# Score products of the first attention as 64-row tiles, three products for each head

## The reference

```python
lat = layer_norm(latents, ln_lat_g, ln_lat_b)
ctx = layer_norm(context, ln_ctx_g, ln_ctx_b)
q = (lat @ Wq)                       # 16 heads of 64
k, v = jnp.split(ctx @ Wkv, 2, axis=-1)
k = apply_rope(k, cos[None, None], sin[None, None])
attn = jnp.einsum('bhnd,bhsd->bhns', q, k) * DHEAD ** (-0.5)
attn = jax.nn.softmax(jnp.clip(attn, -11.0, 11.0), axis=-1)
out = jnp.einsum('bhns,bhsd->bhnd', attn, v)
return out @ Wo + bo
```

## Time and profile before

| | |
|---|---|
| time, median of 3 runs | 3606.59 us (3606.55 to 3608.03) |
| span of the profiled execution, first to last instruction | 3601.8 us |
| instructions | 38810 |
| TensorE, products | 2645.3 us busy (73%) |
| VectorE | 2401.7 us (67%) |
| ScalarE | 1384.5 us (38%) |
| GpSimd | 1429.5 us (40%) |
| mean granted TensorE clock | 0.882 of full |
| first attention's scores | 1024 products, 295.1 us busy |

### The profile page before, as it was taken

The page is one execution under the profiler, slowest core; times in us unless marked ns, Lnnn a source line. Parts: engine busy times, 40 slices in busy tenths (PEclk is TensorE's granted clock), DMA queues, the critical chain, the costliest instruction groups (busy, mean ns, idle before and its releaser), DMA issues. The chain is left out here.

```text
span 3601.8 us, 38810 instructions
## 1 busy us (share of the span) xinstructions
PE 2645.3 (73%) x11472; PEld 1632.8 (45%) x11472; DVE 2401.7 (67%) x3617; ACT 1384.5 (38%) x1913; POOL 1429.5 (40%) x1019
## 2 busy tenths in 40 slices
PE   3987987997996867887788778777877354646465
PEld 3555554554553754544454445444544222323232
DVE  4886786787785764666466646664665586877775
ACT  2553552552552004544354425543553231313121
POOL 3663662563562012343334324432443253443434
PEclk9998998998998877999999889998999676767676
DMA  2010010010101120000000000000000100000000
GB/s 57 14 31 22 14 31 17 15 35 1 30 9 36 47 59 14 13 5 27 22 14 5 27 21 14 5 27 21 14 5 0 38 12 5 25 0 29 0 18 6
DMA packets 109968, 70.48 MB, mean 20 GB/s; under 512 B 15011, under 2 KB 109795, under 8 KB 109795
## 3 DMA queue, kind: packets, MB, share of 16 engines
q1 hardware_dynamic: 109796, 68.44, 6.4%
HBM read 60.03 MB, written 8.39 MB: 19 GB/s over the span
## 5 line engine op out<-in xcount | busy, mean ns | idle before, releaser
L726 ACT ACTIVATE cross_probs<-cross_scores 128x1024 f32<-128x1024 f32 x256 | 259.3, 1024 | 379.8 <-PE cross_scores L938 376.8
L852 DVE TENSOR_REDUCE cross_part<-cross_ring 128x1 f32<-128x512 f32 x512 | 333.0, 686 | 78.4 <-PE cross_ring L1013 75.2
L726 ACT ACTIVATE latent_probs<-latent_scores 128x1024 f32<-128x1024 f32 x256 | 259.1, 1025 | 226.1 <-PE latent_scores L938 202.9
L1013 PE MATMUL cross_ring<-cross_S,cross_Q 128*128 128x512 f32 x512 | 219.3, 475 | 152.9 <-DVE cross_part L852 77.5
L938 PE MATMUL latent_scores<-latent_Q,latent_S 128*128 128x512 f32 x1024 | 295.1, 422 | 28.2 <-issue 17.8
L938 PE MATMUL cross_scores<-cross_Q,cross_S 128*128 128x512 f32 x1024 | 297.7, 420 | 6.0 <-ACT cross_probs L726 2.6
L1046 PE MATMUL latent_outT<-latent_probs,latent_VN 128*64 128x512 f32 x1024 | 264.6, 625 | 15.5 <-DVE latent_probs L873 15.3
L1046 PE MATMUL cross_outT<-cross_probs,cross_VN 128*64 128x512 f32 x1024 | 270.4, 629 | 0.0
L482 POOL TENSOR_TENSOR cross_acc<-cross_probs 128x1024 f32<-128x1024 f32 x32 | 79.8, 2493 | 437.7 <-ACT cross_probs L726 437.7
L482 POOL TENSOR_TENSOR latent_acc<-latent_acc,latent_probs 128x1024 f32<-128x1024 f32 x64 | 153.7, 2402 | 229.0 <-DVE latent_probs L873 229.0
L938 PEld LDWEIGHTS latent_scores<-latent_Q,latent_S 128*128 128x128 f32 x1024 | 191.3, 199 | 111.9 <-issue 53.4
(11 more groups left out here) (300 smaller groups left out, 6531.7 us busy)
## 6 DMA issues: line engine op xcount, KB each, us to landing
latent_WRAW<-in_L_xattn_Wkv_dram SPq DMA_DIRECT2D x64, 128.0 KB, 2.3
latent_C<-in_ctx_dram SPq DMA_DIRECT2D x4, 1024.0 KB, 6.4
latent_WRAW<-in_L_xattn_Wq_dram SPq DMA_DIRECT2D x32, 128.0 KB, 2.3
cross_C<-in_ctx_dram SPq DMA_DIRECT2D x4, 1024.0 KB, 8.6
cross_WRAW<-in_L_xattn_Wq_dram SPq DMA_DIRECT2D x32, 128.0 KB, 2.3
cross_WRAW<-in_L_xattn_Wk_dram SPq DMA_DIRECT2D x32, 128.0 KB, 2.4
cross_WRAW<-in_L_xattn_Wv_dram SPq DMA_DIRECT2D x32, 128.0 KB, 2.3
latent_XN<-in_x_dram SPq DMA_DIRECT2D x4, 512.0 KB, 3.9
```

The lines of the kernel that those rows point to most:

```text
L726: nc.scalar.activation(probs[h][c % 2][:, :, :], scores[h][:, :, :], ACT.Exp).then_inc(exp_done, 1)
L852: nc.vector.reduce_max(part[:, h, qt, i:i + 1], bank[:, :], AX.X).then_inc(taken, 1)
L1013: nc.tensor.matmul(bank[:, :], Q1[nxt][:, h, qt * P:(qt + 1) * P], S1[nxt][:, h, i * 512:(i + 1) * 512], start=True, stop=True).then_inc(f ...
```

## The change

For the latent layer alone, S1, S2, Q1 and Q2 become tiles of 128 partitions for both heads together: high parts in S1 and Q1, low parts in S2 and Q2, head 0 on partitions 0 to 63 and head 1 on 64 to 127. One ScalarE operation copies the whole bank and one VectorE operation subtracts, for kT and for q; the second copy of the queries and the four memsets of zeros are gone. The score products of both heads are issued together at head 1's place: for each key tile three products for each head, 64 rows deep, the two heads in turn, 12 in a chunk. They wait for both exps of the chunk before. At head 0's place the latent layer issues none.

```diff
-        S1 = [sb(f"S1{i}", [P, 2, KEYS], f32r) for i in range(2)]
-        S2 = [sb(f"S2{i}", [P, 2, KEYS], f32r) for i in range(2)] if shifted else S1
-        Q1 = [sb(f"Q1{i}", [P, 2, NQ], f32r) for i in range(2)]
-        Q2 = [sb(f"Q2{i}", [P, 2, NQ], f32r) for i in range(2)]
+        by_head = [2] if shifted else []
+        S1 = [sb(f"S1{i}", [P, *by_head, KEYS], f32r) for i in range(2)]
+        S2 = [sb(f"S2{i}", [P, *by_head, KEYS], f32r) for i in range(2)]
+        Q1 = [sb(f"Q1{i}", [P, *by_head, NQ], f32r) for i in range(2)]
+        Q2 = [sb(f"Q2{i}", [P, *by_head, NQ], f32r) for i in range(2)]
...
-        MADE = {"latent": 9, "cross": 10, "self": 12}[kind]
+        MADE = {"latent": 5, "cross": 10, "self": 12}[kind]
...
@@ ScalarE
+                    elif latent and u in ("kT", "q"):
+
+                        dst = S1[nxt][:, item[1] * 512:item[1] * 512 + 512] if u == "kT" else Q1[nxt][:, :]
+                        nc.scalar.activation(dst, bank[:, :], ACT.Copy).then_inc(high, 1)
@@ VectorE
+                    elif latent and u in ("kT", "q"):
+
+                        cols = slice(item[1] * 512, item[1] * 512 + 512) if u == "kT" else slice(0, NQ)
+                        hi, lo = (S1[nxt], S2[nxt]) if u == "kT" else (Q1[nxt], Q2[nxt])
+                        dve.wait_ge(high, place["kT"] + place["q"] + 1)
+                        nc.vector.tensor_tensor(lo[:, cols], bank[:, :], hi[:, cols].bitcast(fp32), ALU.subtract)\
+                          .then_inc(taken, 1)
@@ TensorE, "S"
                         pe.wait_ge(exp_done, place.attends.value * (2 * NC) + (2 * c + h - 1 + AHEAD))
-                        for k in range(2):
+                        for k in range(2 * latent * h):
+
+                            ks = slice((2 * c + k) * P, (2 * c + k + 1) * P)
+                            for i, (s, q) in enumerate(((S1, Q1), (S1, Q2), (S2, Q1))):
+                                for g in range(2):
+                                    last = nc.tensor.matmul(scores[g][:, k, :], s[par][MAIN[g], ks], q[par][MAIN[g], :],
+                                                            start=i == 0, stop=i == 2)
+                                    if (k, i) == (1, 2):
+                                        last.then_inc(s_full, 1)
+                        for k in range(2 * shifted):
```

More of the change, by code:

```diff
@@ L447, in copies @@
         def copies(place):
-            return place["q"] + place["k"] + place["kT"] if shifted else place["q"]
+            return place["q"] + place["k"] + place["kT"]
         def norm_count(place):
@@ L565, in _ @@
                 nc.gpsimd.memset(spread[:, :].bitcast(fp32), 1.0 / DH).then_inc(const_made, 1)
-            for i in range(2):
+            for i in range(2 if shifted else 0):
                 for h in range(2):
-                    tile, value = (S2[i], 1.0) if shifted else (Q2[i], 0.0)
-                    pool.wait_ge(const_made, 4 + shifted + 2 * i + h)
-                    nc.gpsimd.memset(tile[AUX[h], h, :].bitcast(fp32), value).then_inc(const_made, 1)
+                    pool.wait_ge(const_made, 5 + 2 * i + h)
+                    nc.gpsimd.memset(S2[i][AUX[h], h, :].bitcast(fp32), 1.0).then_inc(const_made, 1)
             pool.wait_ge(const_loaded, 16 * CONSTANTS)
@@ L1024, in do @@
                             evacuated(pe, made if h else made0)
-                        if c == 0 and h == 0:
+                        if shifted and c == 0 and h == 0:
                             pe.wait_ge(copied, copies(place))
                         pe.wait_ge(exp_done, place.attends.value * (2 * NC) + (2 * c + h - 1 + AHEAD))
-                        for k in range(2):
+                        for k in range(2 * latent * h):
[7 more added lines that the diff above has]
+                        for k in range(2 * shifted):
                             ks = slice((2 * c + k) * P, (2 * c + k + 1) * P)
@@ L1032, in do @@
                                                                 (S2[par][:, h, ks], Q2[par][:, h, :])])
-                        last.then_inc(s_full, 1)
+                            if k:
+                                last.then_inc(s_full, 1)
                     elif u == "AV":
```

## The result

The changed kernel takes 3620.08 us (median of 6 runs, 3615.79 to 3620.96), the kernel before 3606.57 us beside it (6 runs, 3603.73 to 3608.37). The ratio is 1.0034 with an interval of 1.0023 to 1.0046: slower by a third of a percent. The forecast was 3586 us, faster. The time lies inside the range of 3562 to 3628, but on the wrong side of no change.

The account below looks back on a forecast made before the run. A loop through all engines was taken to bound the step. Ordinary steps 13.2, norms' steps 6, batch ends 4, first steps -4 and head 1.5 make 20.7 us: 3606.6 to 3586 us, range 3562 to 3628.

Parts of the forecast that it names:

- What bounds the kernel: Latent layer's step: a loop through all engines sets it, TensorE waiting for GpSimd's rotated keys, 57.1 us in all.
- The products and switches: Score products on TensorE: 1.36 for 1.81 us a chunk, one added shape switch of 0.10; 1.4 us a step less work.
- (b): Score products: the row halves overlap only partly, 0.30 us a pair, chunk 1.9; 3592 to 3606 us, chance 0.12.
- (d): Score products: row halves do not overlap, chunk 2.71 + 0.10 us; about 3658 us, chance 0.15.
- (e): Score products: halves overlap but weight loads are not hidden, 0.41 us a pair; about 3635 us, chance 0.05.
- Copies and splits: ScalarE and VectorE: a step saves 3.0 and 2.1 us; the loop shortens by 1.1 us.
- T+3.65: Predicted start of VectorE's clip of chunk 3, in us after the step's key transposes (kT) start; T+4.77 before.
- What gets later: Head 0's product, now behind the unit: costs nothing in ordinary steps, 1 us at each of four batches' first steps.
- The KR pair: GpSimd's last two additions making rotated keys, at the end of the step's loop: taken as 2.86 us.
- The clock: TensorE's granted clock: longer waits drop it to half in one step of three, costing 0.47 us a step.
- Rival (c): TensorE's clock falls in every step because each wait for rotated keys is longer; about 3605 us, no change, chance 0.13.
- waits that I don't see: Remaining chance of 0.05, for waits anywhere in the kernel that the prediction had not seen; no size given.

Follow-up runs that it names:

- unit first: The changed kernel with head 0's products and exp moved behind the preparation unit, right ahead of head 1's: 3581.3 us, 0.9925 of the kernel before.
- half splits: unit first with copies and splits of keys and queries again in two operations of 64 partitions: a step is 26.54 for 25.75 us.
- the kernel before with unit first and no query wait: Kernel before with full-row products, only the plan's order changed and the query-copy number read at the step's start: 3586.6 us, 0.9944.
- two products: unit first without the product of low keys and high queries, 8 products a chunk instead of 12: 10 us slower than with them.

## Why the prediction was wrong

**What bounds the kernel: right.** The loop through all engines sets the step: TensorE still waits for KR in every ordinary step, 0.8 to 0.9 us (before 1.4 to 1.6 in all but two). Where TensorE's work fell by a third of its score products the kernel got slower, and row halves alone shortened no step.

**The products and switches: right.** Twelve products and two switches of shape were counted as 1.36 + 0.2 us a chunk; from 404.58 to AV's start at 406.17 it is 1.59. Rivals (b), (d) and (e) fall. The weight loads are hidden: six pairs with twelve loads of 64 rows start as fast as six full products.

**Copies and splits: right in kind, too large by a third.** 0.79 us a step for 1.1 (unit first against half splits). The clip of chunk 3 came at T+3.90 for T+3.65.

**What gets later: this is the step that failed.** The text says: "In an ordinary step that costs nothing", and "ScalarE waits in order at the first exp, so evacuations queue behind it; the ring's banks taken before it are free, so there is no standstill". The first half names the mechanism and the second dismisses it. It looked at the bank ahead of the exp and not at the two behind: the query that waits in its bank holds VectorE's split, the split holds clips and rotation, and the rotation holds the bank that TensorE wants for the second kv unit, 1.32 us in an ordinary step and 4.54 in one with norms. Moving the exp alone gives 0.81 us in an ordinary step (0.16 in the first of a batch), 2.7 in the norms' step, 1.2, 2.3 and 2.2 in the three behind it, 11.0 us a batch, 36 us of the kernel. I had counted 1 us at each batch's first step, 4 in all.

**A term that the sum did not have.** The KR pair was carried as 2.86 us, a property of GpSimd. It is a property of when VectorE's clip starts against it, and the change happened to move that by half a microsecond. KR starts 2.42 us behind the first product of chunk 2 in both kernels (418.98 to 421.40 before, 425.80 to 428.22 after); the clip starts 2.33 behind it before and 2.90 after, since head 0's scores are complete with the eleventh of twelve products and not with the fourth of eight. That gave back 1.0 us a step. That all of it reaches the step is seen beside the kernel before with unit first and no query wait: from the end of one pair to the start of the next it takes 24.56 us, as before, so the 1.0 us that its step is shorter is the pair. In the changed kernel this rest takes 24.70: the joint splits and the late exp nearly cancel. For an ordinary step the terms are 27.42 - 1.0 (KR) - 0.79 (splits) + 0.81 (exp) = 26.44, and 0.11 for the row halves makes 26.55, measured 26.56. The splits and the exp were measured in the good order and not in the changed one, so that they add up is taken, not shown. Without the shorter pair the change would have cost some 19 us more, an estimate from the 19 pairs of the layer that took 2.84 to 2.92 us before and take 1.86 after.

**The clock.** The ordinary steps kept 1.00, where one dip in three steps was counted, and the wait at kT was 0.89 us, not 2.1 to 2.4: the time that TensorE saved went into the new wait for the rotation, and the KR pair was shorter. Rival (c) did not occur in the ordinary steps here, but two products shows it, and in the step with norms the clock fell behind the new wait (0.90 over the step, 1.00 before).

**The rivals.** None of them had this cause. The chance of 0.05 "for waits that I don't see" was where it lay, for a wait that the text had seen.

**Luck.** With the exp moved the kernel takes 3583.8 us, close to the forecast of 3586. That is not the sum coming true. By the reciprocals the ordinary steps and the last batch gain 26.7 us, where the sum had 13.2: it lacked the KR pair, had the splits too large, and counted dips of the clock that did not come. The three steps with norms gain 5.3 for 6, the batch ends and starts nothing (0.4 us lost). The layer gains 31.9 us for 20.7, and the unchanged layers behind it take 10.5 us longer in that trace.

**The count of steps.** The sum takes 21 ordinary steps, six of them of 26.1 to 26.4 us. Between the reciprocals of the kernel before there are sixteen distances of 27.4 to 27.5 us and only two of the shorter kind, in the last batch; the three steps behind those with norms, counted with them, have 41.9. With 18 the term is 11.3 us and not 13.2.

## What to carry to other kernels

When a product is moved in one engine's order, every consumer that keeps its place can become a barrier in its own queue: follow what stands behind it, engine by engine, until it comes back to the engine that sets the pace. Move the exp with its products; that alone made the difference between 0.3 percent slower and 0.6 percent faster. A duration in a trace is a fact of what ran beside it: before carrying it into a sum, ask whether the change moves its neighbour.

## What was unexpected of the hardware

- Products of the two row halves run entirely at once not only when they alternate but also three and three (1.68 us for twelve); six and six take 2.22, one half alone 1.65 for six.
- Fewer products can cost time: two for three made a kernel 10 us slower, through a clip that came 0.5 us earlier behind the chunk's first product (2.44 for 2.90 us) and a clock at 0.52 behind a wait of 2.64 us.
- GpSimd's add of 128 x 256 took 0.73 us alone and 1.66 beside VectorE; the order of two starts 0.5 us apart changed a pair by 1.0 us.
